# Graph network kernel: the six edge gather passes with their loops written out on four engines

## What is computed

```python
# L0, three times: relative messages, maximum over the edges of a node
e = relu((x[dst] - x[src]) @ theta.T + x[src] @ phi.T)
x = batchnorm_relu(segment_max(e, src))
# L1, twice: a weight matrix per edge type, weighted mean over the edges
weight = einsum('rb,bio->rio', att, basis)
H = einsum('ni,rio->nro', x, weight)
agg = segment_sum(H[src, et] * ea[:, None], dst) / cnt[:, None]
h = relu(layernorm(x + agg + x @ root + bias))
# L2, once: graph convolution
agg = segment_sum((x @ W)[src] * norm[:, None], dst)
# L3, once: attention over the edges, then an MLP
scores = einsum('ehd,ehd->eh', q[src], k[dst])
agg = segment_sum(v[src] * softmax_by_dst(scores), dst)
```

## Time and profile before

| | |
|---|---|
| median of 3 runs | 6430.61 us (6429.56 to 6430.99) |
| span of the profiled execution | 7532.0 us, 76440 instructions |
| PE, busy | 3093.3 us, 41% |
| PEld, busy | 1810.4 us, 24% |
| DVE, busy | 3776.4 us, 50% |
| ACT, busy | 1789.8 us, 24% |
| POOL, busy | 3184.4 us, 42% |
| DMA | 1064.44 MB, mean 141 GB/s |

### The profile page before, as it was taken

The page is one execution under the profiler, slowest core; times in us unless marked ns, Lnnn a source line. Parts: engine busy times, 40 slices in busy tenths (PEclk is TensorE's granted clock), DMA queues, the critical chain, the costliest instruction groups (busy, mean ns, idle before and its releaser), DMA issues. The chain is left out here.

```text
span 7532.0 us, 76440 instructions
## 1 busy us (share of the span) xinstructions
PE 3093.3 (41%) x12803; PEld 1810.4 (24%) x12803; DVE 3776.4 (50%) x9366; ACT 1789.8 (24%) x4594; POOL 3184.4 (42%) x3188
## 2 busy tenths in 40 slices
PE   4474000433335455579500089200120016677648
PEld 3332000311113222244200044000110013555425
DVE  8995444444445555544455342333543344555553
ACT  1173000111111455421122221222210002222212
POOL 0002666334442656400366510566446654444440
PEclk9997555655556677789755599655555558888869
DMA  0002454323332444323455543455434545777730
GB/s 7 0 0 93 148 173 168 119 91 134 134 134 88 147 150 159 131 93 153 142 170 192 176 149 140 145 174 174 144 127 167 185 152 166 255 253 250 255 98 18
DMA packets 379735, 1064.44 MB, mean 141 GB/s; under 512 B 74258, under 2 KB 162612, under 8 KB 333012
## 3 DMA queue, kind: packets, MB, share of 16 engines
q1 hardware_dynamic: 213586, 595.68, 20.8%
q0 software_dynamic: 164688, 466.32, 20.8%
q10 hardware_dynamic: 1330, 0.99, 0.0%
HBM read 541.40 MB, written 521.29 MB: 141 GB/s over the span
## 5 line engine op out<-in xcount | busy, mean ns | idle before, releaser
L789 POOL DMA_INDIRECT out_of<-table,index x936 | 937.5, 1002 | 981.4 <-DVE index L813 710.8
L789 POOL DMA_INDIRECT rows<-table,index x728 | 725.7, 997 | 411.3 <-issue 229.2
L789 POOL DMA_INDIRECT rows<-typed_table,index x520 | 513.8, 988 | 638.1 <-DVE index L813 484.7
L3110 POOL DMA_INDIRECT qv<-qv_table,index x416 | 420.9, 1012 | 447.9 <-DVE index L3310 322.8
L789 POOL DMA_INDIRECT y<-typed_table,index x312 | 322.7, 1034 | 622.3 <-DVE index L813 531.5
L1494 PE MATMUL bank<-x,marks 128*128 128x416 f16 x1664 | 391.5, 401 | 366.4 <-ACT marks L1508 278.0
L828 DVE SCALAR_TENSOR_TENSOR y<-y,by_source_anew,out_of 128x256 f32<-128x256 f32 x897 | 433.9, 484 | 159.5 <-issue 32.2
L1508 ACT ACTIVATE marks<-hot_block,x 128x128 f16<-128x128 f16 x1248 | 371.6, 387 | 393.2 <-DVE marks L1549 362.5
L2163 PE MATMUL bank<-weights,turned_y 128*128 128x512 f32 x800 | 357.5, 596 | 5.5 <-ACT turned_y L2223 5.5
L3187 PE MATMUL bank<-weighed_rows,hot 128*128 128x272 f32 x832 | 283.8, 467 | 176.8 <-ACT y L3285 93.2
L1964 PE MATMUL bank<-weights,out_of 128*128 128x512 f32 x800 | 349.7, 595 | 13.2 <-DVE weights L2012 13.2
(11 more groups left out here) (586 smaller groups left out, 7684.4 us busy)
## 6 DMA issues: line engine op xcount, KB each, us to landing
states<-y SPq DMA_DIRECT2D x156, 1024.0 KB
typed_table<-staged SPq DMA_DIRECT2D x400, 256.0 KB, 2.0
states<-state SPq DMA_DIRECT2D x78, 1024.0 KB
states<-out_of SPq DMA_DIRECT2D x78, 1024.0 KB
wide_states<-y SPq DMA_DIRECT2D x52, 1088.0 KB
near<-k_rows SPq DMA_DIRECT2D x416, 128.0 KB
out_of<-table,index POOLq DMA_INDIRECT x936
rows<-table,index POOLq DMA_INDIRECT x728
```

Source lines behind the costliest of these rows:

```text
L789: pool.indirect_dma_start(out=rows[h][:, u * D:(u + 1) * D], out_offset=None, in_=table, in_offset=bass.IndirectOffsetOnAxis(ap=index[h][: ...
L3110: pool.indirect_dma_start(out=qv[b][:, u * PAIR:(u + 1) * PAIR], out_offset=None, in_=qv_table, in_offset=bass.IndirectOffsetOnAxis(ap=ind ...
```

## The change

Every `Fori` of VectorE, ScalarE, TensorE and SyncE in the six edge passes and in their companions becomes a Python loop: all 52 groups are written out with constant addresses. With this go the register arithmetic, the waits against registers and the increments of `held` on these engines (the companions' `held` and `mix_held` semaphores go with them). GpSimd's loop in `edge_pass` stays as it is. The order of the instructions on each engine and the values that they wait for stay the same. The diff, cut to its core:

```diff
@@ -798,35 +798,31 @@
             if fold == "weighted":
                 @block.scalar
                 def _(act):
-                    with act.Fori(0, rounds) as i:
+                    for i in range(rounds):
                         for h in range(RING):
                             act.wait_ge(gathered[h], (i + 1) * (16 * GROUP))
-                            act.sem_inc(held, 1)
                             for u in range(GROUP):
                                 row = rows[h][:, u * D:(u + 1) * D]
-                                nc.scalar.activation(row, row, ACT.Copy, scale=order.weight[:, bass.ds((RING * i + h) * GROUP + u, 1)]
+                                nc.scalar.activation(row, row, ACT.Copy, scale=order.weight[:, (RING * i + h) * GROUP + u:(RING * i + h) * GROUP + u + 1]
                                                      ).then_inc(weighed, 1)
 
             @block.vector
             def _(dve):
                 def look(g, h):
-                    nc.vector.tensor_copy(index[h][:], index_of[:, bass.ds(g * GROUP, GROUP)]).then_inc(indexed, 1)
+                    nc.vector.tensor_copy(index[h][:], index_of[:, g * GROUP:(g + 1) * GROUP]).then_inc(indexed, 1)
 
                 def fold_group(i, h, more=True, alone=False, mix=False):
                     g = RING * i + h
                     dve.wait_ge(gathered[h], (i + 1) * (16 * GROUP))
-                    dve.sem_inc(held, 1)
-                    if not isinstance(i, int) or i > 0:
+                    if i > 0:
                         dve.wait_ge(stored[h], i * 16)
-                        dve.sem_inc(held, 1)
                     for u in range(GROUP):
                         before = state[h][:, (u - 1) * D:u * D] if u else state[h - 1][:, (GROUP - 1) * D:]
                         if fold == "weighted":
                             dve.wait_ge(weighed, g * GROUP + u + 1)
-                            dve.sem_inc(held, 1)
                         dve.wait_ge(chain, g * GROUP + u + 1)
                         nc.vector.scalar_tensor_tensor(
-                            out=state[h][:, u * D:(u + 1) * D], in0=before, scalar=marks[:, bass.ds(g * GROUP + u, 1)],
+                            out=state[h][:, u * D:(u + 1) * D], in0=before, scalar=marks[:, g * GROUP + u:g * GROUP + u + 1],
                             in1=rows[h][:, u * D:(u + 1) * D], op0=op0, op1=op1).then_inc(chain, 1)
                     if more:
                         look(g + RING, h)
@@ -852,13 +848,9 @@
                     beside.ahead(dve)
                     for h in range(RING):
                         beside.group(dve, h, h % 2)
-                if mixing:
-                    with dve.Fori(1, mixed_rounds) as i:
-                        for h in range(RING):
-                            fold_group(i, h, mix=True)
-                with dve.Fori(mixed_rounds, rounds - 1) as i:
+                for i in range(1, rounds - 1):
                     for h in range(RING):
-                        fold_group(i, h)
+                        fold_group(i, h, mix=i < mixed_rounds)
                 for h in range(RING):
                     fold_group(rounds - 1, h, more=False)
                 dve.wait_ge(chain, STEPS + 1)
@@ -874,18 +866,16 @@
 
                 def store(i, mix=False):
                     for h in range(RING):
+                        at = (RING * i + h) * (GROUP * D)
                         sp.wait_ge(chain, (RING * i + h + 1) * GROUP + 1)
-                        sp.sem_inc(held, 1)
-                        sp.dma_start(blocks[:, bass.ds((RING * i + h) * (GROUP * D), GROUP * D)], state[h][:, 0:GROUP * D]).then_inc(stored[h], 16)
+                        sp.dma_start(blocks[:, at:at + GROUP * D], state[h][:, 0:GROUP * D]).then_inc(stored[h], 16)
                         if mix and h == RING - 2:
                             mixing.file(sp, i)
 
                 if mixing:
                     mixing.load(sp)
-                    with sp.Fori(0, mixing.rounds) as i:
-                        store(i, mix=True)
-                with sp.Fori(mixing.rounds if mixing else 0, rounds) as i:
-                    store(i)
+                for i in range(rounds):
+                    store(i, mix=bool(mixing) and i < mixing.rounds)
                 if mixing:
                     sp.wait_ge(mixing.filed, 16 * mixing.rounds)
                 for h in range(RING):
@@ -1029,28 +1019,22 @@
                         rectify(c)
 
 
-def over_groups(engine, body):
-
-
-    for h in range(2):
-        body(h, h)
-    with engine.Fori(1, GROUPS // 2 - 1) as i:
-        for h in range(2):
-            body(2 * i + h, h)
-    for h in range(2):
-        body(GROUPS - 2 + h, h)
+def over_groups(body):
+
+    for g in range(GROUPS):
+        body(g, g % 2)
 
 
 def hot_blocks(nc, env, out, columns, g):
 
     return nc.vector.tensor_tensor(out=bulk(out, GROUP), in0=env.iota_p[:].unsqueeze(1).broadcast_to([P, GROUP, P]),
-                                   in1=columns[:, bass.ds(g * GROUP, GROUP)].unsqueeze(2).broadcast_to([P, GROUP, P]), op=ALU.is_equal)
+                                   in1=columns[:, g * GROUP:(g + 1) * GROUP].unsqueeze(2).broadcast_to([P, GROUP, P]), op=ALU.is_equal)
 
 
 def hot_tiles(nc, env, out, columns, g):
 
     return nc.vector.tensor_tensor(out=bulk(out, GROUP), in0=env.iota_a1[:].unsqueeze(1).broadcast_to([P, GROUP, TILES]),
-                                   in1=columns[:, bass.ds(g * GROUP, GROUP)].unsqueeze(2).broadcast_to([P, GROUP, TILES]), op=ALU.is_equal)
+                                   in1=columns[:, g * GROUP:(g + 1) * GROUP].unsqueeze(2).broadcast_to([P, GROUP, TILES]), op=ALU.is_equal)
 
 
 class Lent:
...
@@ -1109,17 +1093,15 @@
             def body(g, h):
                 if later(g):
                     pe.wait_ge(copied, g - 1)
-                    pe.sem_inc(held, 1)
-                nc.tensor.transpose(turn_bank[h][:, 0:P], sort.z[:, bass.ds(g * P, P)], env.ident16[:]).then_inc(turned, 1)
+                nc.tensor.transpose(turn_bank[h][:, 0:P], sort.z[:, g * P:(g + 1) * P], env.ident16[:]).then_inc(turned, 1)
                 pe.wait_ge(hot, 2 * g + 2)
-                pe.sem_inc(held, 1)
                 for u in range(GROUP):
                     last = nc.tensor.matmul(env.bank[2][:, 0:TILES], self.hot_b[h][:, u * P:(u + 1) * P], self.hot_a[h][:, u * TILES:(u + 1) * TILES],
-                                            start=isinstance(g, int) and g == 0 and u == 0,
-                                            stop=isinstance(g, int) and g == GROUPS - 1 and u == GROUP - 1)
+                                            start=g == 0 and u == 0,
+                                            stop=g == GROUPS - 1 and u == GROUP - 1)
                 last.then_inc(tallied, 1)
             pe.wait_ge(bits_made, 4 + 3 * NODE_BITS + 2)
-            over_groups(pe, body)
+            over_groups(body)
             pe.wait_ge(summed, 1)
             nc.tensor.matmul(env.bank[3][:, 0:TILES], env.after[:], order.count[:], start=True, stop=True)
             nc.tensor.matmul(env.bank[4][:, 0:TILES], env.ones[:], order.count[:], start=True, stop=True).then_inc(totalled, 1)
@@ -1128,9 +1110,8 @@
         def _(act):
             def body(g, h):
                 act.wait_ge(turned, g + 1)
-                act.sem_inc(held, 1)
-                nc.scalar.copy(sort.z[:, bass.ds(g * P, P)], turn_bank[h][:, 0:P]).then_inc(copied, 1)
-            over_groups(act, body)
+                nc.scalar.copy(sort.z[:, g * P:(g + 1) * P], turn_bank[h][:, 0:P]).then_inc(copied, 1)
+            over_groups(body)
 
     def ahead(self, dve):
         nc, sort, order, part = self.sort.nc, self.sort, self.sort.order, self.part
...
@@ -1291,34 +1271,28 @@
         @block.tensor
         def _(pe):
             def compare(g, h):
-                now = sort.z[:, bass.ds(g * P, P)]
+                now = sort.z[:, g * P:(g + 1) * P]
                 pe.wait_ge(self.masked, g + 1)
-                pe.sem_inc(self.held, 1)
                 for s in range(2):
-                    if not isinstance(g, int) or g > 0:
+                    if g > 0:
                         pe.wait_ge(self.compared, 2 * g + s - 1)
-                        pe.sem_inc(self.held, 1)
                     nc.tensor.matmul(self.alike_bank[s][:, 0:half], now, self.mine[h][:, s * half:(s + 1) * half],
...
@@ -1479,36 +1432,33 @@
         self.cut = [self.sort.order.anew[:].bitcast(I32), self.sort.env.tmp[:].bitcast(I32)]
 
     def share(self, block, sems):
-        self.step, self.hot, self.marked, self.used, self.held = sems
+        self.step, self.hot, self.marked, self.used = sems
         nc, env = self.sort.nc, self.sort.env
 
         @block.tensor
         def _(pe):
             def body(g, h):
                 pe.wait_ge(self.hot, g + 1)
-                pe.sem_inc(self.held, 1)
                 pe.wait_ge(self.marked, g + 1)
-                pe.sem_inc(self.held, 1)
```

(20 more changed lines are left out.)

68 lines of the change are left out of this document (20 added, 48 removed).

## The result

The changed kernel takes 6482.67 us (median of 4 runs, 6478.39 to 6487.72), the kernel before 6430.8 us: ratio 1.0074, 95% interval 1.0062 to 1.0086. It is 52 us slower, where no change or a small gain was forecast, and lies 31 us above the range.

The account below looks back on a forecast made before the run. The prediction took GpSimd's gathers to bound the passes in timed runs, hiding most VectorE savings. Its terms, 2.6 + 0.5 + 2.0 + 0.9 + 0.9 + 0.4 + 0.2 = 7.5 us, gave 6423.1 us from 6430.6; range 6345 to 6452.

Parts of the forecast that it names:

- 1.25 us, whether or not anything else is late: GpSimd's gathers in the edge passes: each takes 0.95 us, the next comes 0.30 us later, so 520 us a pass.
- The waits as an effect of the record: GpSimd's steady waits for `index`, 685 us in six passes, come from recording instructions at about 0.7 us each.
- the budget of 1008 against 1101 us: Steady GpSimd waits, 1008 us with the attention pass, are less than the 1101 us by which timed runs were shorter.
- The profiled span: Whole kernel under profiling: fewer recorded instructions give 425 us back, so a span near 7110 us, 6950 to 7300.
- Head of pass 2, 2.6 us: Pass 2's companion before fold 4: groups at 8.13 and 8.69 us become 7.13 us, a gain of 2.6 us.
- a first fold's 0.65 us: First looped fold after a late head in passes 1, 2 and 6: 0.65 us gained each, 2.0 us together.
- The small terms for the pass ends: Pass ends: SyncE's last store 0.9 us, ScalarE's weighing in passes 4 and 5 0.4, fewer semaphores to clear 0.2.
- Folds 0.52 us apart throughout: VectorE's folds in the passes would come at 0.52 us a step throughout instead of 0.62.
- Copies of pass 3: ScalarE's 24 copies in pass 3's companion take 7.11 us written out or looped: no gain.
- Rival B: Straight code arrives late in passes 2 and 3: +29 us, 6452 us (6440 to 6480); chance 0.14.
- A: Rival: part of GpSimd's waits is real, 16 to 80 us gained, about 6375 us (6340 to 6408); chance 0.28.
- C: Rival: the waits are all real and VectorE is the bound, 214 us come out, 6216 us; chance 0.02.

Follow-up runs that it names:

- the change with halves: The changed kernel with `hot_blocks` and the product into `marks` each as two half-length VectorE instructions: 7240.7 and 7263.82 us, where the kernel before takes 7510 to 7515 us.
- the version with true spacing: The changed kernel with one VectorE semaphore increment between the wait for the last fold and the next fold: 6442.71 us, 1.0017 against the kernel before.

## Why the prediction was wrong

- **The step that failed: "1.25 us, whether or not anything else is late".** The whole sum rests on a gather of constant length, taken from one row, so that faster folds could cost nothing and everything that they win is hidden. The gathers are 393.5 us of a pass's 520 only when VectorE leaves their starts alone. In the passes before, they are 147 us longer in all (2508.4 - 6 x 393.5), after 205 us. The missing term, put at nothing in the sum, is the lengthening of gathers by VectorE's placement: +53 us, 29 by the folds and 24 by `hot_b`. It was to be read from the first page of before, where the mean of one gather is 1002 ns in the largest group and not 946; I took a gather of a quiet stretch instead. The mean shows that gathers are lengthened, not what the change would do to it; the sign came only from laying starts over instructions. The rule of the Trainium skill on the shared ports was the rival to draw from it, and none of mine had it. The row stood there:

```profile
L789 POOL DMA_INDIRECT out_of<-table,index x936 | 937.5, 1002 | 981.4 <-DVE index L813 710.8
```

- **The waits as an effect of the record: right in what it gave, wrong in its reason.** GpSimd does run at its own pace in an undisturbed execution: outside pass 2 its waits are gone, and the span is within 9 us of the median. But the comparison of 7532 us with 6431 us was one between two conditions of the machine, not between recording and none; timed runs in that condition take 7510 us too. The argument from the budget of 1008 against 1101 us proved nothing.
- **The profiled span** near 7110 us: 6476.6 us came, in the undisturbed condition. In the other, the change with halves has 7245 and 7256 us: 287 and 276 us less than 7532, where 425 were expected. Pass 2 returned 113 us (830 to 717), near the 120 forecast; passes 4 to 6 returned 120 us where the forecast had 73 + 90 + 59 = 222.
- **Head of pass 2, 2.6 us and a first fold's 0.65 us**: GpSimd's one wait there fell from 25.7 to 21.5 us, 4.2 us, where the two terms give 3.25. The mechanism was right, the size a little low: the companion's two looped groups took 8.01 and 8.71 us before and 5.76 and 6.53 us after, 4.4 us less and not 2.6, from the starts of line 1433 (1389 after). The small terms for the pass ends (folds' first to last against the gathers') can't be told from the rest; outside the passes the change has 4 us less (48.7 - 53).
- **Folds 0.52 us apart throughout**: seen in passes 1, 2, 3 and 6, and it is what costs; in passes 4 and 5 it is 0.589 us. **Copies of pass 3**: ScalarE's busy time is unchanged (356.99 and 356.86 us).
- **Rival B, code fetched late**, had the right sign and, by its upper end of 6480 us, nearly the size, but not the cause. The packets grew as bounded (85 to 126, 46 to 72; 67 more, half of the doubling), and no wait in the passes answers to them; the version with true spacing has more packets still (137 and 72) and takes 40 us less. The choice of 0 for the fetch stands. **A and C** fall with the 7532 us.
- **The range** ended at 6452 us, since its upper side came from B alone. A mechanism that I had not priced at all lay outside it.

## What to carry to other kernels

Where GpSimd's gathers set the pace, read the spread of their durations first: a mean above the minimum was here mostly time lent to VectorE, and it is found by laying the gathers' starts over VectorE's instructions with two SBUF inputs. Then make those instructions short (halves of 1.2 us ones, 42 us off one pass) rather than the others fast; a faster engine off the path can still cost by where its work comes to lie, and a period near a fraction of the gathers' period (2 x 0.62 in 1.25 us) can be worth more than a shorter one. Where each instruction will lie was not foreseen in any run here, so such a change has to be measured. And compare a profiled span with the timed median only after a second record of the same kernel.

## What the runs showed of the hardware that was not expected

- A gather of 128 rows takes 0.946 us and 0.305 us between; held by a two-input VectorE instruction, it ends 0.82 us after that instruction's end. Beside the operations over 6400 columns (6.82 us) single gathers last 6.55 to 6.79 us in before, and up to 7.59 us in other runs.
- Looped folds and gathers lock into each other: in pass 6, 44 of 48 groups have one gather held, mostly by 0.09 to 0.14 us, and most of those after it start 0.37 to 0.40 us into a fold and go free. In passes 3 to 5 about half of the groups or more have none held.
- The same alignment isn't stable: `hot_b` of pass 1 costs 2.4 us in the kernel before and 26.2 us with only TensorE's and ScalarE's code written out. What flips it was not found.
- Some 7 us of longer gathers at the head of pass 1 are there in every run, before and after alike, and are not told by the rule above: 11 or 12 gathers are 0.55 to 0.69 us longer beside the instruction of 1.04 us at line 1145, with one input, which starts 0.34 to 0.44 us after the gather does. It was not followed.
- A semaphore increment of VectorE costs the folds nothing while one of them is running, and 0.11 us between two folds when it stands behind the wait (0.632 against 0.521 us; in passes 4 and 5 0.617 against 0.589).
- The machine has a condition in which engines, where held up, go by steps of 0.7 us and this kernel takes 17% longer.
